# Adaptive-layernorm network with a chunked scan: half of each scan step's output projection moved into the step's own matrix work

## The chip, the core and the metric

The kernel runs on one NeuronCore of a Trainium2 chip. The core has a matrix engine (TensorE; PE in the profile, with its weight loads as PEld), a vector engine (VectorE, DVE), a scalar engine (ScalarE, ACT) and a general one (GpSimd, POOL). Each takes its own list of instructions in order and waits on semaphores; DMA queues move data beside them. The metric is the device time of one execution in microseconds. Before the change the median of three runs is 800.75 us (795.25 to 800.98).

## What is computed

Eight sequences of 512 tokens with 128 channels pass through two layers. Layer 0 is a state-space filter and a mixture of experts, layer 1 a chunked scan and a second mixture of experts. The change is in the scan of layer 1, and in the output projection that follows it:

```python
def step(carry, xs):                       # one chunk of 64 tokens
    W_in, W_out = carry
    qi, ki, vi, li, lo, wi, wo = xs
    p_q = softmax(einsum('bnhd,bDhd->bnhD', qi, W_in), axis=1)
    o = einsum('bnhD,bDhd->bnhd', p_q, W_out)
    p = softmax(einsum('bnhd,bDhd->bnhD', ki, W_in), axis=1)
    grad_out = einsum('bnhD,bnhd->bDhd', -p, vi)
    a = einsum('bDhd,bnhd->bnhD', W_out, vi)
    s = sum(p * a, axis=-1, keepdims=True)
    g_z = -(p * a - p * s)
    grad_in = einsum('bnhd,bnhD->bDhd', ki, g_z)
    W_in = wi * W_in - li * grad_in
    W_out = wo * W_out - lo * grad_out
    return (W_in, W_out), o
...
x = x + ga * (o @ Wo.T)                    # the projection that is split
```

## The kernel before

Everything is fp32 on 128 partitions. The eight sequences go in four pairs (`BP` = 4), each pair's 64-token chunk filling 128 partitions, so the scan has `T` = 32 steps: 8 chunks of 4 pairs, a chunk's four pairs one after the other. Each pair has its own states `w_in` and `w_out`. The first `TU` = 28 steps run in one software pipeline, written out by hand; the last four have no update and end apart. Each engine has a hand-written order of calls; nothing is scheduled by a program. The instruction list of the scan is unrolled.

PSUM is four banks of 1024 columns, `ps[0]` to `ps[3]`, all in use: `ps[0]` takes the values, then the output o, then `a`, then `grad_in`; `ps[1]` the half `[:, 0:128]` for the projection y, then q, then `grad_out`, then the turned values; `ps[2]` the turned keys, the turned `w_out`, then half of the logits; `ps[3]` k, the turned softmax weights, then the other half of the logits.

PE's loop over i runs in this order (in brackets the line of the profile): `y_of(i-3)`, the eight matmuls of the output projection of an earlier step (L1973); in three of four steps a small helper for the next chunk (`group_turn` L1892, `group_tokens` L1899, `group_sum` L1906 and L1909; none after step 21 or so, save one turn); `project` for the values and for q (L1918); `grad_in` (L1980); `k_turn` (L1951); `project` for k (L1918); `states_turn` (L1959); `states_q`, which makes o (L1966); `grad_out` (L1988); `p_turn`, the turn of the softmax weights (L1951); `a_of`, the pass of the values through `w_out` (L2009); `v_turn` (L1951); `logits_of` twice (L2018). Each fp32 matmul stands in the trace as two MATMUL and two LDWEIGHTS records, so the eight of `y_of` are x16. Those of 128x128 tiles are long, those of 64x64 tiles short.

Between a step's `a_of` and the next `project` of the values lies a loop through another engine: both write `ps[0]`, and DVE reads it in `weigh` (L1474), `mean` (L1478) and `difference` (L1482), which sets `am_done`. PE waits for it before that `project`, and POOL's `make_g` (L623) waits for it too, whose product `grad_in` needs.

DVE's order in one turn is `mean`, `difference`, `maxima` (L1443), `gate_y` (L1497), `group_rates_out` in one of four, `maxima`, `centre` twice (L1449), `add_up` (L1455), `update_in` (L1492), `q_silu` (L1433), `add_up`, `k_silu` (L1439), `invert` (L1462), `update_out` (L1487), in two of four a measurement for a layernorm (L1374 and L1378, or L1407 and L1412), `weigh`. POOL's is `scale_k` (L598), `normalise_p` twice (L619), `decay_out` (L584), `make_g` (L623), `decay_in` (L584), `add_y` (L628), `scale_v` (L598), with gathers and group work between. `gate_y` multiplies y by the gate into `y_gated`, and `add_y` adds it to x. ACT's `oT_of` (L989) copies o out of PSUM, and `w_outT_out` (L984) the turned states.

Of the kernel before, what the change touches and what calls it, by code (L numbers as in the profile page):

```python
# [5 lines left out]
ALU = mybir.AluOpType  # L6
# [7 lines left out]
P = 128  # L14
# [55 lines left out]
def program(nc, A):  # L70
    ctx = ExitStack()
    with ctx:
# [3 lines left out]
        def sem(name):  # L76
            return ctx.enter_context(nc.semaphore(name))
# [21 lines left out]
        def view(at, n, dt=F32):  # L99
# [106 lines left out]
        w_in = [view(23552 + 2048 * bp, 1024) for bp in range(BP)]  # L206
        w_out = [view(24576 + 2048 * bp, 1024) for bp in range(BP)]
        y_gated = small[:, 128:256]
        z_max = small[:, 256:288]
        z_sum, z_rec = ([small[:, 288 + 64 * k + 32 * u:320 + 64 * k + 32 * u] for u in range(2)] for k in range(2))  # L210
        s_sum, junk = small[:, 416:432], small[:, 432:433]
# [29 lines left out]
            sem(n) for n in ("z_centered", "z_summed", "pk_norm", "pq_norm", "silu_q", "silu_k", "g_done", "wout_new", "y_scaled", "win_new"))  # L241
        z_exp, vT_out, tanh_q, tanh_k, vtok_out, ktok_out, ptok_out, oT_out, woutT_out = (
            sem(n) for n in ("z_exp", "vT_out", "tanh_q", "tanh_k", "vtok_out", "ktok_out", "ptok_out", "oT_out", "woutT_out"))
        v_scaled, k_scaled, wout_dec, win_dec, x_added = (sem(n) for n in ("v_scaled", "k_scaled", "wout_dec", "win_dec", "x_added"))
        h_stored = [sem(f"h_stored{u}") for u in range(2)]
        lg_mm, tiles_counted, ex_done, oh_done, cnt_done, rhs_ready, ids_mm, gw = (
# [54 lines left out]
        def tile_of(t):  # L301

            return t % BP * NC + t // BP
# [12 lines left out]
        def y_bank(t):  # L316
            n = t - TU
            return ps[1][:, 0:C] if n < 0 else ps[2][:, n % 2 * 512:n % 2 * 512 + C]
# [142 lines left out]
        def _(pool):  # L461
# [144 lines left out]
            def scale_k(t):  # L606
                pool.wait_ge(ktok_out, t + 1)
                pool.wait_ge(group_rates, t // BP + 1)
                rate(k_tok, 0, t, k_scaled)
# [11 lines left out]
            def make_g(t):  # L621
                pool.wait_ge(am_done, t + 1)
                pool.tensor_tensor(g_tok, g_tok, p_tok, ALU.mult).then_inc(g_done, 1)  # L623

            def add_y(t):
                pool.wait_ge(y_scaled, t + 1)
                x = x_sb[:, tile_of(t) * C:(tile_of(t) + 1) * C]
                pool.tensor_tensor(x, x, y_gated, ALU.add).then_inc(x_added, 1)  # L628

# [21 lines left out]
            for i in range(-1, TU - 1):  # L651
                if 3 <= i and i + 17 < T:
                    gather_back(i + 17)
                if (c := group_of(i, 10, 3)) is not None:
                    group_add(c)
                if i >= 0:
                    scale_k(i)
                normalise_p(i + 1, 0, pq_norm)
                normalise_p(i + 1, 1, pk_norm)
                if i < 3:  # L660
                    gather_back(2 * i + 14)
                    gather_back(2 * i + 15)
                if i >= 0:
                    decay_out(i)
                if i >= 0:
                    make_g(i)
                if i >= 0:
                    decay_in(i)
                if i >= 0:
                    add_y(i)  # L670
                if (c := group_of(i, 12, 3)) is not None:
                    group_gate(c)
                if i >= 0:
                    scale_v(i)
                if (c := group_of(i, -11, 0, NC - 4)) is not None:
                    second_scale(c)
                if (c := group_of(i, -13, 0, NC - 4)) is not None:
                    second_shift(c)
            second_scale(NC - 4)
            scale_k(TU - 1)  # L680
            second_shift(NC - 4)
            normalise_p(TU, 0, pq_norm)
            decay_in(TU - 1)
# [411 lines left out]
        def _(dve):  # L1095
# [393 lines left out]
            def update_in(t):  # L1489
                dve.wait_ge(pe_gin, t + 1)  # L1490
                dve.wait_ge(win_dec, t + 1)
                dve.tensor_tensor(w_in[t % BP], w_in[t % BP], ps[0], ALU.add).then_inc(win_new, 1)  # L1492

            def gate_y(t):
                dve.wait_ge(pe_y, t + 1)
                after(dve, x_added, t)
                dve.tensor_tensor(y_gated, y_bank(t), rows1(GA, t % BP), ALU.mult).then_inc(y_scaled, 1)  # L1497
# [28 lines left out]
            for i in range(-1, TU - 1):  # L1526
# [26 lines left out]
                    group_measure(c)  # L1553
                if (c := group_of(i, -5, 0, NC - 2)) is not None:
                    second_measure(c)
                weigh(i + 1)
            mean(TU - 1)
            difference(TU - 1)
# [144 lines left out]
        def _(pe):  # L1703
# [265 lines left out]

            def y_of(t):  # L1970
                pe.wait_ge(oT_out, t + 1)
                for n in range(HP):
                    mm = pe.matmul(y_bank(t), oT_buffer(t)[:, n * P:(n + 1) * P], w_o[:, n * C:(n + 1) * C], start=(n == 0), stop=(n == HP - 1))  # L1973
                mm.then_inc(pe_y, 1)

            def grad_in(t):
                pe.wait_ge(g_done, t + 1)
# [109 lines left out]
            for i in range(2, TZ):  # L2087
# [42 lines left out]
                    grad_out(i - 3)  # L2130
                pe.wait_ge(silu_k, i + 1)
                p_turn(i - 2)
                a_of(i - 2)
                if i == 2:
                    pe.wait_ge(silu_q, i + 1)
# [1 line left out]
                v_turn(i - 2)  # L2137
                pe.wait_ge(silu_q, i + 1)
                pe.wait_ge(silu_k, i + 1)
                if i < TU:  # L2140
                    logits_of(i, 0)
                    after(pe, ptok_out, i - 1)
                    logits_of(i, 1)
                else:
                    last_logits(2 * i - TU)
                    if i < TZ - 1:
                        pe.wait_ge(ptok_out, i - 1)
                        last_logits(2 * i - TU + 1)
# [186 lines left out]
```

## Time and profile before

| | |
|---|---|
| median of three runs | 800.75 us (795.25 to 800.98) |
| the profiled execution, whole | 804.12 us |
| its span in the trace | 802.4 us |
| PE busy | 713.5 us, 89% of the span |
| PE weight loads busy | 655.1 us, 82% |
| DVE busy | 626.5 us, 78% |
| POOL busy | 580.9 us, 72% |
| ACT busy | 476.7 us, 59% |
| chain that ended last | PE 68%, DVE 10%, issue 8% |
| mean granted TensorE clock | 0.938 of full |

The scan of the 28 updated steps lies between about 161 us and 684 us. The trace gives for each instruction a start and a duration and, for idle time before it, what ended the wait; "issue" stands where the profile shows nothing that was waited for. Ends of matmuls are modelled, so lengths of PE's work are best read from one start to the next. A projection's x16 row and the next row's start, for example, tell what it took.

### The profile page before, as it was taken

How to read it: one execution, taken by the hardware profiler on the slowest of the kernel's cores; microseconds unless marked ns; L12 is line 12 of the kernel's file. 1: busy time of each engine (PE TensorE's matmuls, PEld its weight loads, DVE VectorE, ACT ScalarE, POOL GpSimd, SP SyncE). 2: the span in 40 equal slices, each digit the busy share in tenths (PEclk: the TensorE clock that was granted, in tenths of full speed). 3: DMA queues.
4: the chain of work that ended last, by engine and by line, in shares of the span. 5: the costliest groups of instructions: out<-in, count | busy, mean ns of one | idle time of the engine just before them, and what ended most of it. 6: DMA issues, size and time to landing. Idle time of an engine off the chain costs nothing.

```text
span 802.4 us, 34232 instructions
## 1 busy us (share of the span) xinstructions
PE 713.5 (89%) x14919; PEld 655.1 (82%) x14920; DVE 626.5 (78%) x1033; ACT 476.7 (59%) x774; POOL 580.9 (72%) x433
## 2 busy tenths in 40 slices
PE   5679798678899999999999999999999999877997
PEld 5357587577799989898888989898988889776897
DVE  6594645379789989899898999999998899866205
ACT  5673244238755756686676678667657775641930
POOL 7630377276979898889888988889787888832750
PEclk8695689979999999999999999999999999986999
DMA  8402334310520000000000000000000000061127
GB/s 324 197 28 77 102 77 103 69 30 9 160 68 14 6 7 7 10 7 7 7 7 7 19 4 2 18 3 3 3 17 4 3 15 18 5 227 65 52 82 273
DMA packets 33584, 42.89 MB, mean 53 GB/s; under 512 B 4001, under 2 KB 25649, under 8 KB 32929
## 3 DMA queue, kind: packets, MB, share of 16 engines
q1 hardware_dynamic: 29856, 33.99, 12.6%
q0 software_dynamic: 3296, 6.76, 3.5%
q8 instruction: 117, 1.92, 1.0%
q14 instruction: 27, 0.21, 0.1%
q10 hardware_dynamic: 288, 0.01, 0.0%
HBM read 26.65 MB, written 14.09 MB: 51 GB/s over the span
## 4 chain that ended last, share of the span: by engine, by line
PE 68%; DVE 10%; issue 8%; ACT 6%; DMA 5%; POOL 2%; POOLq 0%; ACTq 0%; SPq 0%; DVEq 0%
PE psum L1918 19%; PE psum L1973 7%; PE psum L1951 7%; PE psum L2018 7%; PE psum L2009 4%; PE psum L1966 4%; PE psum L1980 4%; PE psum L1988 3%; DMA arena<-h_rows,route 2%; PE psum L1959 2%; ACT arena L1076 2%; POOL arena L560 2%; PE psum L2276 2%; ACT arena L1086 1%; PE psum L1777 1%
## 5 line engine op out<-in xcount | busy, mean ns | idle before, releaser
L1918 PE MATMUL psum<-hT,w_qkv 128*128 128x128 f32 x1408 | 176.3, 283 | 2.6 <-DVE arena L1395 1.4
L1918 PEld LDWEIGHTS psum<-hT,w_qkv 128*128 128x128 f32 x1408 | 166.7, 196 | 5.8 <-DVE arena L1395 1.6
L619 POOL TENSOR_TENSOR arena<-arena,small 128x1024 f32<-128x1024 f32 x56 | 106.0, 1914 | 41.2 <-DVE small L1462 41.2
L598 POOL TENSOR_TENSOR arena<-arena 128x1024 f32<-128x1024 f32 x56 | 106.6, 1904 | 10.6 <-ACT arena L973 10.4
L584 POOL TENSOR_TENSOR arena<-arena 128x1024 f32<-128x1024 f32 x56 | 106.6, 1904 | 0.1
L1455 DVE TENSOR_REDUCE small<-arena 128x16 f32<-128x1024 f32 x60 | 73.0, 1217 | 8.9 <-ACT arena L962 6.8
L623 POOL TENSOR_TENSOR arena<-arena 128x1024 f32<-128x1024 f32 x28 | 65.9, 2355 | 13.5 <-DVE arena L1482 13.5
L1443 DVE TENSOR_REDUCE small<-psum 128x16 f32<-128x1024 f32 x60 | 72.7, 1213 | 0.0
L1449 DVE TENSOR_TENSOR arena<-psum,small 128x1024 f32<-128x1024 f32 x60 | 70.4, 1212 | 0.1
L942 ACT ACTIVATE arena<-psum 128x1024 f32<-128x1024 f32 x28 | 28.7, 1024 | 69.6 <-PE psum L1918 69.6
L560 POOL DMA_INDIRECT arena<-h_rows,route x39 | 39.6, 1016 | 39.7 <-issue 38.4
L1951 PE MATMUL psum<-arena 64*128 64x64 f32 x1344 | 61.8, 230 | 6.7 <-issue 3.9
L2018 PE MATMUL psum<-arena 64*64 64x128 f32 x1792 | 61.5, 279 | 5.6 <-issue 2.8
L1973 PE MATMUL psum<-w_o,arena 128*128 128x128 f32 x512 | 65.1, 281 | 0.6 <-ACT arena L989 0.6
L962 ACT ACTIVATE arena<-arena 128x1024 f32<-128x1024 f32 x60 | 62.9, 1051 | 4.5 <-DVE arena L1449 4.2
L1973 PEld LDWEIGHTS psum<-w_o,arena 128*128 128x128 f32 x512 | 60.0, 193 | 4.5 <-issue 3.4
L1951 PEld LDWEIGHTS psum<-arena 64*128 64x128 f32 x1344 | 49.4, 139 | 12.8 <-issue 3.9
L2018 PEld LDWEIGHTS psum<-arena 64*64 64x64 f32 x1792 | 51.9, 136 | 9.6 <-issue 7.4
L947 ACT ACTIVATE arena<-psum 128x1024 f32<-128x1024 f32 x28 | 28.7, 1025 | 36.1 <-PE psum L1951 31.9
L1474 DVE TENSOR_TENSOR arena<-arena,psum 128x1024 f32<-128x1024 f32 x28 | 34.0, 1216 | 18.6 <-PE psum L2009 18.2
L546 POOL DMA_INDIRECT arena<-o_rows,route x32 | 33.1, 1034 | 19.9 <-DMA o_rows<-arena 13.2
L875 ACT ACTIVATE arena<-psum,route 128x128 f32<-128x128 f32 x78 | 21.3, 380 | 41.9 <-PE psum L1856 41.9
(332 smaller groups left out, 1625.6 us busy)
## 6 DMA issues: line engine op xcount, KB each, us to landing
y_rows<-hT SPq DMA_DIRECT2D x8, 512.0 KB
arena<-in_L_W_rows SPq DMA_DIRECT2D x2, 2048.0 KB, 11.3
arena<-y_rows SPq DMA_DIRECT2D x8, 512.0 KB, 8.8
o_rows<-arena SPq DMA_DIRECT2D x9, 256.0 KB
x_sb<-in_x_rows SPq DMA_DIRECT2D x4, 512.0 KB, 6.0
arena<-in_L_W_rows SPq DMA_DIRECT2D x2, 1024.0 KB, 9.9
arena<-in_W_in_rows SPq DMA_DIRECT2D x4, 512.0 KB, 14.9
arena<-in_W_out_rows SPq DMA_DIRECT2D x4, 512.0 KB, 9.6
```

Of the source, the lines that this page charges most:

```text
L584: pool.tensor_tensor(w4, w4, d4.unsqueeze(3).to_broadcast([P, 2, HP, D]), ALU.mult).then_inc(done, 1)
L598: pool.tensor_tensor(x3, x3, lr[:, tile_of(t) * 32 + k * H:tile_of(t) * 32 + k * H + H].unsqueeze(2).to_broadcast([P, H, D]), ALU.mult).th ...
L619: pool.tensor_tensor(z4, z4, r3.unsqueeze(3).to_broadcast([P, 8, 2, CH]), ALU.mult).then_inc(done, 1)
L623: pool.tensor_tensor(g_tok, g_tok, p_tok, ALU.mult).then_inc(g_done, 1)
L962: act.activation(z, z, ACT.Exp, scale=0.5).then_inc(z_exp, 1)
L1443: dve.tensor_reduce(z_max[:, 16 * jh:16 * jh + 16], h3(ps[2 + jh]), AX_X, ALU.max).then_inc(z_maxed, 1)
L1449: dve.tensor_tensor(h3(zs[t % 2][:, jh * 1024:(jh + 1) * 1024]), h3(ps[2 + jh]), z_max[:, 16 * jh:16 * jh + 16].unsqueeze(2).to_broadcast( ...
L1455: dve.tensor_reduce(z_sum[t % 2][:, 16 * jh:16 * jh + 16], h3(zs[t % 2][:, jh * 1024:(jh + 1) * 1024]), AX_X, ALU.add).then_inc(z_added, 1)
L1918: mm = pe.matmul(ps[bank][:, p * P:(p + 1) * P], w_qkv[:, j * HD + p * P:j * HD + (p + 1) * P], hT[:, at:at + P], start=True, stop=True)
L1951: mm = pe.transpose(out[:, col((r, 2), (n, HP))], of[half(r), at(n):at(n) + P], eye[half(r), :])
L1973: mm = pe.matmul(y_bank(t), oT_buffer(t)[:, n * P:(n + 1) * P], w_o[:, n * C:(n + 1) * C], start=(n == 0), stop=(n == HP - 1))
L2018: mm = pe.matmul(out, w_in[t % BP][half(r), col((be, 2), (p, HP))], x4[half(r), :, p, be, :], start=True, stop=True)
```

## The change

In steps below `TU` the output projection is split. `y_of` does the second four of its eight matmuls, at its old place and into its old bank. A new `early_y_of` does the first four between `p_turn` and `a_of` of the step itself, into `ps[2][:, 0:C]`, after ACT has copied the turned states out of that bank. DVE's new `gate_early_y` multiplies this half by the gate into a new buffer `early_gated` (128 columns of SBUF), ahead of `weigh`. POOL's new `add_early_y` adds it to x, between `scale_k` and `normalise_p`; `add_y` then adds the second half. PE waits for `early_scaled` before `logits_of` writes the bank again. Three semaphores of layer 0 are used anew.

```diff
+        early_gated = sb("early_gated", [P, C])[:, :]
...
+        early_y, early_scaled, early_added = a0_up, a0_scaled, a0_sq
...
+            def add_early_y(t):
+                pool.wait_ge(early_scaled, BP + t + 1)
+                x = x_sb[:, tile_of(t) * C:(tile_of(t) + 1) * C]
+                pool.tensor_tensor(x, x, early_gated, ALU.add).then_inc(early_added, 1)
+
             def add_y(t):
                 pool.wait_ge(y_scaled, t + 1)
+                pool.wait_ge(early_added, BP + min(t + 1, TU))
...
                     scale_k(i)
+                if i >= 0:
+                    add_early_y(i)
                 normalise_p(i + 1, 0, pq_norm)
...
             scale_k(TU - 1)
+            add_early_y(TU - 1)
...
+            def gate_early_y(t):
+                dve.wait_ge(early_y, BP + t + 1)
+                dve.wait_ge(early_added, BP + t)
+                dve.tensor_tensor(early_gated, ps[2][:, 0:C], rows1(GA, t % BP), ALU.mult).then_inc(early_scaled, 1)
...
+                gate_early_y(i + 1)
                 weigh(i + 1)
...
             def y_of(t):
                 pe.wait_ge(oT_out, t + 1)
-                for n in range(HP):
-                    mm = pe.matmul(y_bank(t), oT_buffer(t)[:, n * P:(n + 1) * P], w_o[:, n * C:(n + 1) * C], start=(n == 0), stop=(n == HP - 1))
+                n0 = HP // 2 if t < TU else 0
+                for n in range(n0, HP):
+                    mm = pe.matmul(y_bank(t), oT_buffer(t)[:, n * P:(n + 1) * P], w_o[:, n * C:(n + 1) * C], start=(n == n0), stop=(n == HP - 1))
                 mm.then_inc(pe_y, 1)
+
+            def early_y_of(t):
+                pe.wait_ge(oT_out, t + 1)
+                pe.wait_ge(woutT_out, t + 1)
+                for n in range(HP // 2):
+                    mm = pe.matmul(ps[2][:, 0:C], oT[:, n * P:(n + 1) * P], w_o[:, n * C:(n + 1) * C], start=(n == 0), stop=(n == HP // 2 - 1))
+                mm.then_inc(early_y, 1)
...
                 p_turn(i - 2)
+                early_y_of(i - 2)
                 a_of(i - 2)
...
                 pe.wait_ge(silu_k, i + 1)
+                pe.wait_ge(early_scaled, BP + i - 1)
                 if i < TU:
                     logits_of(i, 0)
```

PE's order of the kernel before, in a step in the middle of the scan, from `grad_out` to the next step's projections of the values and of q:

```order
L1988 MATMUL psum<-arena 64x64 x32
L1951 MATMUL psum<-arena 128x64 x16
L2009 MATMUL psum<-arena 64x64 x32
L1951 MATMUL psum<-arena 128x64 x16
L2018 MATMUL psum<-arena 64x2x64 x32
L1892 MATMUL psum<-ident,arena 128x128 x4
L1973 MATMUL psum<-w_o,arena 128x128 x8
L1918 MATMUL psum<-hT,w_qkv 128x128 x16
```

The same place after the change, where L1998 is `early_y_of`, L1991 `y_of`, L2034 `a_of` and L2043 `logits_of`:

```order
L2013 MATMUL psum<-arena 64x64 x32
L1968 MATMUL psum<-arena 128x64 x16
L1998 MATMUL psum<-w_o,arena 128x128 x4
L2034 MATMUL psum<-arena 64x64 x32
L1968 MATMUL psum<-arena 128x64 x16
L2043 MATMUL psum<-arena 64x2x64 x32
L1909 MATMUL psum<-ident,arena 128x128 x4
L1991 MATMUL psum<-w_o,arena 128x128 x4
L1935 MATMUL psum<-hT,w_qkv 128x128 x16
```

Four long matmuls have gone from behind the logits to a place ahead of `a_of`, of the step before in the pipeline's count; the number of matmuls is the same.

DVE's order of the kernel before around `weigh` (L1474), in a step with a layernorm measurement:

```order
L1462 RECIPROCAL small<-small 128x32
L1487 TENSOR_TENSOR arena<-arena,psum 128x1024
L1374 BN_STATS small<-x_sb 128x6 x4
L1378 BN_AGGR small<-small 128x2 x4
L1474 TENSOR_TENSOR arena<-arena,psum 128x1024
L1478 TENSOR_REDUCE small<-arena 128x16
L1482 TENSOR_TENSOR arena<-psum,small 128x1024
```

The same place after the change, where L1508 is `gate_early_y` and L1485 `weigh`:

```order
L1473 RECIPROCAL small<-small 128x32
L1498 TENSOR_TENSOR arena<-arena,psum 128x1024
L1385 BN_STATS small<-x_sb 128x6 x4
L1389 BN_AGGR small<-small 128x2 x4
L1508 TENSOR_TENSOR early_gated<-psum,mod 128x128
L1485 TENSOR_TENSOR arena<-arena,psum 128x1024
L1489 TENSOR_REDUCE small<-arena 128x16
L1493 TENSOR_TENSOR arena<-psum,small 128x1024
```

One small operation is new, just ahead of `weigh`; `gate_y` stays where it was.

## Rows read from the trace of the kernel before

**Rows 1.** Windows of every engine: start:end, length, busy time of each (instructions), clock, DMA.

```profile
241.03:598.06 357.03, 343.50 (x9083) 320.42 (x9081) 331.40 (x417) 244.31 (x323) 313.73 (x189) 1.00 0.03 8
598.06:684.68 86.62, 82.89 (x2311) 77.59 (x2309) 78.78 (x85) 56.58 (x67) 73.41 (x44) 1.00 0.04 10
```

**Rows 2.** PE's timeline, step from 598 us: start, length, line, operation, count, [idle before].

```profile
598.06 2.05 PE L1973 MATMUL psum<-w_o,arena 128*128 128x128 f32 x16
599.95 3.74 PE L1918 MATMUL psum<-hT,w_qkv 128*128 128x128 f32 x32
603.61 1.16 PE L1980 MATMUL psum<-arena 64*64 64x64 f32 x64
...
610.65 1.04 PE L2009 MATMUL psum<-arena 64*64 64x64 f32 x56
612.58 0.34 PE L2009 MATMUL psum<-arena 64*64 64x64 f32 x8 [0.88 <-issue]
612.85 0.72 PE L1951 MATMUL psum<-arena 64*128 64x64 f32 x16
...
615.40 0.66 PE L1892 MATMUL psum<-ident,arena 128*128 128x128 f32 x4
615.90 0.72 PE L1973 MATMUL psum<-w_o,arena 128*128 128x128 f32 x5
```

**Rows 3.** PE's timeline, the other two helpers and what follows them.

```profile
421.46 1.00 PE L1899 MATMUL psum<-arena,hT 128*128 128x64 f32 x8
422.31 3.79 PE L1918 MATMUL psum<-hT,w_qkv 128*128 128x128 f32 x32
...
439.99 0.39 PE L1906 MATMUL psum<-arena 128*128 128x128 f32 x2
...
440.69 0.49 PE L1918 MATMUL psum<-hT,w_qkv 128*128 128x128 f32 x2
```

**Rows 4.** Waits from 220 to 690 us: total us, times, longest us.

```profile
PE psum L2009 <- issue: 7.4, 11, 1.1
...
PE psum L1951 <- issue: 3.9, 7, 0.8
PE psum L2018 <- issue: 2.8, 6, 0.6
...
PE psum L1988 <- issue: 1.8, 2, 1.2
```

**Rows 5.** PE's timeline at two gaps that follow each other.

```profile
290.30 0.21 PE L1951 MATMUL psum<-arena 64*128 64x64 f32 x1 [0.68 <-issue]
...
294.06 0.87 PE L2018 MATMUL psum<-arena 64*64 64x128 f32 x19 [0.36 <-issue]
```

**Rows 6.** Window of every engine between those two gaps, columns as in rows 1.

```profile
290.30:294.06 3.76, 3.40 (x126) 2.89 (x126) 2.42 (x3) 2.05 (x2) 3.76 (x3) 1.00 0.02 4
```

**Rows 7.** The page's part on DMA queues: packets, MB, share.

```profile
q8 instruction: 117, 1.92, 1.0%
```

**Rows 8.** DVE's timeline, weigh, difference and gate_y in four steps.

```profile
435.66 1.22 DVE L1474 TENSOR_TENSOR arena<-arena,psum 128x1024 f32<-128x1024 f32 x1 [1.49 <-PE psum L2009]
...
438.17 1.22 DVE L1482 TENSOR_TENSOR arena<-psum,small 128x1024 f32<-128x1024 f32 x1
...
453.34 1.19 DVE L1474 TENSOR_TENSOR arena<-arena,psum 128x1024 f32<-128x1024 f32 x1
...
470.12 1.22 DVE L1474 TENSOR_TENSOR arena<-arena,psum 128x1024 f32<-128x1024 f32 x1 [1.14 <-PE psum L2009]
...
475.51 0.29 DVE L1497 TENSOR_TENSOR small<-psum,mod 128x128 f32<-128x128 f32 x1 [0.53 <-PE psum L1973]
...
505.65 1.22 DVE L1474 TENSOR_TENSOR arena<-arena,psum 128x1024 f32<-128x1024 f32 x1 [0.82 <-PE psum L2009]
```

**Rows 9.** POOL's timeline, add_y in one step and make_g in another.

```profile
424.85 0.46 POOL L628 TENSOR_TENSOR x_sb<-x_sb,small 128x128 f32<-128x128 f32 x1
...
439.47 2.35 POOL L623 TENSOR_TENSOR arena<-arena 128x1024 f32<-128x1024 f32 x1 [0.66 <-DVE arena L1482]
```

## The prediction

> **What bounds the kernel now.** I read first the windows of all engines over the scan, cut at the starts of `y_of`. From 241.03 to 598.06 us lie 20 steps, from there to 684.68 five more [rows 1]. A step takes 357.03 / 20 = 17.85 us in the first stretch and 86.62 / 5 = 17.32 in the second, at full clock. PE is busy for 96% of both; DVE is next with 331.40 / 357.03 = 93%. So PE sets the step, and DVE has little over a microsecond to spare.
>
> Next I read PE's timeline of a single step [rows 2]. The step starts with `y_of` at 598.06, the projections of v and q start at 599.95, `a_of` at 610.65, `v_turn` at 612.85, and the logits end at 615.40. `a_of` is cut in two: after 56 of its 64 records PE stood still for 0.88 us, and "issue" means that nothing waited for is seen. `grad_in`, 64 records of the same shape, takes 1.16 at 603.61, some 0.06 of it beside the block behind. So `a_of` would take 1.10, and here it takes 2.20: the stop costs 1.10. Without it the step is 17.34 - 1.10 = 16.24. The helpers add 0.50 (615.40 to 615.90), 0.85 and 0.70 [rows 2, 3] in three of four steps, 0.51 on average. So a step in the first stretch would be 16.75 without stops, against 17.85 found: **1.10 us of each step is such a stop.**
>
> What is it? The list of waits shows where the stops stand: 7.4 us at `a_of`, 2.8 at the logits, 3.9 at the turns, 1.8 at `grad_out` [rows 4], all in the stretch of short matmuls, none at the projections. Two stops that follow each other, at 290.30 and 294.06, each fall inside a block [rows 5], and between them PE took 126 matmul and 126 load records [rows 6]. The queue q8 moved 117 packets of code and 1.92 MB, which is 16 KB a packet [rows 7]. My reading is that a packet holds the next 252 records and a few waits, and that a stop is PE at the end of one packet before the next is in. The stretch from one such stop to the next took 3.76 us, its end stop included. A run that holds a projection takes longer: `project` needs 3.66 / 2 = 1.83 us for 32 records (599.95 to 603.61), against 1.10 for the 128 of `grad_in`. There are no stops at the projections.
>
> The Trainium skill, "Runtime: NRT & Kernel Launch", section "Instruction fetch mechanics", says that each engine's instruction memory is refilled in 16 KiB blocks of 256 instructions while it runs, which these rows agree with, and that the crossing is mostly hidden because the sequencer dispatches more slowly than the blocks arrive. By that half of the rule there is nothing for the change to take away, and the sum below would lose its only gain; rows 5 and 6 do not agree with it for short matmuls, but it is the third rival.
>
> **The change part by part.**
>
> Four matmuls (8 matmul and 8 load records) move from the slow stretch to the middle of the dense one. Half of 1.89 is 0.95 us [rows 2]. A run that holds them takes 0.95 longer, so a stop at its end shrinks by up to 0.95; the stops are 1.10 a step, and the run that `y_of` leaves has the projections and stays long. Not all stops lie behind the new place. Those at `grad_out` (1.8) lie ahead of it, and of the 3.9 at the turns I take 3.2 as `p_turn`'s, ahead of it too (rows do not part `p_turn` from `v_turn`; 0 and 3.9 are the bounds). That is 5.0 of 15.9, 31%. So of 1.10 some 0.34 stay, and 0.02 for stops over 0.95: **0.36 left, 0.74 taken**. Bounds: 0.1 left, or all 1.10.
>
> PE gets three more waits and a second accumulation group. No row shows their price here. Below, nothing; above, 0.32, four times the 0.08 of a semaphore that has to come from another engine (below). I take 0.1 a step, near nothing, since what they wait for is done.
>
> DVE gets one 128x128 operation, 0.29 us as `gate_y` [rows 8]; I take 0.28 a step. POOL gets one of 0.46 us [rows 9]. It is busy for 313.73 of 357.03 us [rows 1], so it has 2.16 idle a step, and what stands behind the new place, `normalise_p`, is used by PE only in the next step. I cost it at nothing; with that cover gone it would be up to 0.46 a step. ACT and the DMA queues get nothing.
>
> **The cover that goes.** PE's next `project` of the values waits for `am_done`. `difference` ends at 438.17 + 1.22 = 439.39, 3.73 behind the start of `weigh` at 435.66 [rows 8]. A semaphore between engines costs 0.08: `make_g`, which waits for the same one, starts at 439.47 [rows 9]. With two of them PE may start 3.9 us after the end of `a_of`. Before, PE had 2.55 (turn and logits, 612.85 to 615.40) and 1.89 (`y_of`) to do, 4.44 and more. Now it has 2.55 + 0.95 = 3.50 and the helper. So a step without a helper waits 0.4 us for DVE, and with a late DVE more. If `weigh` is late by L, PE starts at the greater of 3.50 + helper and 3.90 + L after the end of `a_of`. From that start to the end of the next `a_of` is 10.70 (599.95 to 610.65) + 1.10 + 0.95 = 12.75, plus 0.36 and 0.1, 13.21.
>
> How late DVE is comes from its own work between two `weigh`. The four steps of [rows 8], without the waits for PE, are: with the rates and a measurement 453.34 - 435.66 = 17.68; bare 16.78 - 1.14 = 15.64; the next two 35.53 - 0.53 - 0.82 = 34.18, 17.09 each. With 0.28: 17.96, 15.92, 17.37, 17.37. The waits for `y_of` in `gate_y` go, since half a projection ends sooner.
>
> Four steps in a row, L = 0 at first:
> - helper 0.70: PE starts at 4.20, step 17.41; DVE late by 17.96 - 17.41 = 0.55.
> - no helper: 3.90 + 0.55 = 4.45, step 17.66; DVE catches up.
> - helper 0.50: 4.00, step 17.21; DVE late by 0.16.
> - helper 0.85: 4.35, step 17.56; DVE catches up.
>
> The mean is 69.84 / 4 = 17.46, a gain of 0.39 a step: of 0.74 taken from the stops nearly half goes to DVE and the handshake. Over 20 steps that is 7.8. The five steps behind have almost no helper: 3.90 + 13.21 = 17.11 each, 85.55 against 86.62, a gain of 1.1. The three steps ahead of 241 us are of the first stretch's kind: 1.0. The sum is **9.9 us**. The profiled execution took 804.12, so 794.2; in the same ratio the median of 800.75 becomes **791**.
>
> **The rivals.**
>
> *More relief or less coupling.* If all stops went, the same four steps give 17.31 and 16.75 for bare ones: 10.8 + 2.9 + 1, about 15 us, 786. If the stops are as I say but DVE never holds PE up, a step is 16.75 + 0.46 = 17.21 and a bare one 16.70: 12.8 + 3.1 + 1, about 17, 784. Both together 775. For it: DVE's waits inside a step [rows 8] may shrink further. Against: DVE at 93% now, and at 96% of a step of 17.5.
>
> *The relief is there and is eaten.* Single stops go up to 1.2 us [rows 4] and some steps have none, and DVE's load from 15.6 to 17.7; my four steps use the mean stop. Where a stop and a light step meet, nothing is won. If that costs 0.25 a step, the gain is 4 us: 797.
>
> *Slower: the code fetch is not what stops PE, or a packet costs its fixed time anyway.* Then 1.10 stays, the shorter cover counts, and PE goes from start to end of `a_of` in 12.75 + 1.10 + 0.1 = 13.95. With the same rules steps are 18.15, 17.85, 17.95 and 18.30, mean 18.06, 0.21 worse; bare ones 17.85, 0.53 worse: 4.2 + 2.6 = 6.8, **807.5**. This is decided by the relief: from 0.25 us a step down the change loses. Against it: 252 records between two stops [rows 6] and none at the slow blocks.
>
> **How the numbers follow.** Forecast (787 to 795) 0.50, more relief (775 to 786) 0.18, eaten (795 to 802) 0.20, slower (802 to 812) 0.12. A measurement can tell about 1% from no change, which is 8 us: below 792.7 is faster, above 808.8 slower. Three quarters of the forecast and all of the first rival are below: 0.55. Half of the last is above: 0.06. The rest, 0.39, is within. The range leaves out the farthest of both sides: 780 to 803.
>
> **What would show it.** In the timeline of PE the new four matmuls take 0.95 us and the stops behind them nearly vanish, while those at `grad_out` and `p_turn` stay; their total falls from 1.10 to about 0.36 a step. A new wait of PE at the projection of the values (the line of `project`), released by DVE's `difference`, of about 0.4 in steps without a helper. DVE's wait before `weigh` is mostly gone, and its busy share rises to 96%. `gate_y` no longer waits for `y_of`. No wait of PE at the logits for the early gate. Wrong would be: stops as long as before, or a wait at the logits.

## The result, and the profile after

The changed kernel takes 817.83 us, median of four runs (815.67 to 818.78), against 800.6 us for the kernel before. The ratio is 1.0224, with a 95% interval of 1.0183 to 1.0266: 2.2% slower. The forecast was 791 us in a range of 780 to 803, so it was wrong in sign. Even the rival that had it slower ended at 812.

In the profiled executions the span grew from 802.4 to 817.0 us, by 14.6. The windows of every engine, cut at the same places as [rows 1], show where. First the kernel before, its ending (the last four scan steps) and all that follows; columns are start:end, length, busy time of PE, PEld, DVE, ACT, POOL with instructions, granted clock, DMA.

```profile
684.68:699.32 14.64, 11.33 (x424) 10.29 (x421) 13.76 (x24) 9.77 (x15) 11.61 (x8) 1.00 0.02 4
699.32:802.40 103.08, 86.00 (x751) 81.42 (x751) 44.97 (x116) 41.43 (x117) 41.52 (x41) 0.89 0.39 136
```

The same windows of the changed kernel, with its 20 and 5 steps ahead of them:

```profile
241.25:603.08 361.83, 346.95 (x9085) 322.08 (x9081) 337.18 (x437) 245.38 (x322) 319.58 (x209) 1.00 0.03 8
603.08:690.32 87.24, 83.81 (x2313) 77.76 (x2309) 79.83 (x91) 57.14 (x69) 75.63 (x49) 1.00 0.03 6
690.32:709.97 19.65, 12.67 (x412) 11.50 (x412) 15.70 (x24) 10.36 (x15) 14.71 (x10) 0.79 0.06 16
709.97:817.00 107.03, 91.50 (x751) 87.30 (x751) 44.14 (x116) 41.47 (x117) 41.63 (x41) 0.85 0.38 131
```

The 20 steps took 361.83 us for 357.03 [rows 1], 18.09 a step for 17.85. The five behind took 87.24 for 86.62, the ending 19.65 for 14.64. The rest took 107.03 for 103.08; that part is not the change's, since in a second pair of traces from one chip (e0 and e7 below) it is 104.5 before and 104.0 after.

The waits of the changed kernel between 220 and 700 us (total, times, longest):

```profile
POOL x_sb L630 <- DVE early_gated L1508: 54.7, 25, 3.5
...
DVE arena L1485 <- PE psum L2034: 17.6, 24, 3.4
PEld psum L2005 <- issue: 15.1, 20, 3.8
...
PE psum L2005 <- issue: 11.2, 12, 3.7
...
PEld psum L1968 <- DVE arena L1450: 3.6, 16, 0.5
...
PEld psum L1935 <- DVE arena L1493: 2.4, 6, 0.4
```

Against [rows 4], the stops at `a_of` (now L2034) and at the logits (L2043) no longer stand near the top of PE's waits. PE now waits ahead of `grad_in` (L2005), where [rows 4] has nothing. At the top is GpSimd, standing 54.7 us at the new addition (L630) for VectorE's new gate.

One step of the changed kernel shows how these hang together. These are GpSimd, the new gate, the weigh behind it and TensorE, from the timeline:

```profile
454.99 1.16 PE L1998 MATMUL psum<-w_o,arena 128*128 128x128 f32 x8
...
456.08 1.16 PE L2034 MATMUL psum<-arena 64*64 64x64 f32 x64
...
456.79 0.26 DVE L1508 TENSOR_TENSOR early_gated<-psum,mod 128x128 f32<-128x128 f32 x1
...
457.31 1.22 DVE L1485 TENSOR_TENSOR arena<-arena,psum 128x1024 f32<-128x1024 f32 x1 [0.26 <-PE psum L2034]
457.35 0.46 POOL L630 TENSOR_TENSOR x_sb<-x_sb,early_gated 128x128 f32<-128x128 f32 x1
457.77 3.78 POOL L621 TENSOR_TENSOR arena<-arena,small 128x1024 f32<-128x1024 f32 x2
...
461.10 1.16 PE L1935 MATMUL psum<-hT,w_qkv 128*128 128x128 f32 x8 [0.22 <-DVE arena L1493]
461.52 1.89 POOL L586 TENSOR_TENSOR arena<-arena 128x1024 f32<-128x1024 f32 x1
```

GpSimd's two `normalise_p` (L621) begin only when the early half has been multiplied, gated and added. Behind them come `decay_out` (L586) and `make_g`. In this step GpSimd was busy with its own work until 457.35 and did not stand at the addition. In the step before it did, for 1.97 us, and that step shows what it does to TensorE:

```profile
439.29 0.46 POOL L630 TENSOR_TENSOR x_sb<-x_sb,early_gated 128x128 f32<-128x128 f32 x1 [1.97 <-DVE early_gated L1508]
439.71 3.78 POOL L621 TENSOR_TENSOR arena<-arena,small 128x1024 f32<-128x1024 f32 x2
443.45 1.90 POOL L586 TENSOR_TENSOR arena<-arena 128x1024 f32<-128x1024 f32 x1
...
445.31 2.36 POOL L625 TENSOR_TENSOR arena<-arena 128x1024 f32<-128x1024 f32 x1
...
447.77 1.16 PE L2005 MATMUL psum<-arena 64*64 64x64 f32 x64 [0.61 <-issue]
```

`make_g` (L625) ends at 447.67 and `grad_in` starts at 447.77. In the kernel before, `make_g` of the same step started at 439.47 after an idle time of 0.66 [rows 9] and ended at 441.82, over two microseconds before it was needed. Over the 20 steps `make_g` ends 2.42 us ahead of `grad_in` on average in the kernel before; in the changed kernel `grad_in` starts 0.10 us behind it in 17 of 20 steps.

In the ending nothing hides this:

```profile
690.32 1.16 PE L1991 MATMUL psum<-w_o,arena 128*128 128x128 f32 x8
...
694.96 2.35 POOL L625 TENSOR_TENSOR arena<-arena 128x1024 f32<-128x1024 f32 x1
...
697.41 1.98 PE L2005 MATMUL psum<-arena 64*64 64x64 f32 x64 [3.66 <-issue]
```

TensorE stood 3.66 us for `make_g`, and the granted clock of the ending's window is 0.79, where it was 1.00 before. Cut finer, it is 1.00 until the wait has begun and 0.50 (the 1.2 GHz level) behind it. Columns are start:end, length, busy time of PE with instructions, granted clock, DMA:

```profile
692.00:694.00 2.00, 1.16 (x64) 1.00 0.04 8
...
697.40:699.30 1.90, 1.89 (x64) 0.50 0.00 0
```

The 64 records of `grad_in` took 1.98 us instead of 1.16. Of the 5.01 us that the ending grew, 3.06 lie ahead of the start of `grad_in` (7.09 us from the ending's start for 4.03), and 1.95 between it and the logits behind it (5.03 for 3.08), where the same work ran at the lower clock.

The table sets 20 steps of each kernel side by side. Each figure is the mean length of a block in us, from its start to the next block's start in PE's timeline, so a wait counts to the block ahead of it. The last column is e1, below.

| block of a step | before | changed | e1 |
|---|---|---|---|
| projection y, both halves | 1.86 | 2.15 | 2.12 |
| v and q, and waits ahead of `grad_in` | 3.71 | 4.18 | 3.74 |
| `states_q` and `grad_out`, and waits ahead of the turn | 2.10 | 2.37 | 2.51 |
| `p_turn`, `a_of`, `v_turn`, logits | 5.27 | 4.48 | 4.44 |
| everything else | 4.91 | 4.91 | 4.91 |
| step | 17.85 | 18.09 | 17.72 |

### The profile page after: what moved, and what is told of

Same layout as the page of the kernel before. It is cut to its first block, busy times and chain, and to the rows that moved or that the text cites. A ratio compares the mean times of both kernels' runs of the same rounds, so it can differ in the third digit from the quotient of the medians.

```text
span 817.0 us, 34402 instructions
## 1 busy us (share of the span) xinstructions
PE 722.5 (88%) x14919; PEld 661.4 (81%) x14920; DVE 635.7 (78%) x1061; ACT 479.0 (59%) x774; POOL 592.1 (72%) x461
## 4 chain that ended last, share of the span: by engine, by line
POOL 40%; issue 20%; PE 19%; DVE 13%; ACT 5%; DMA 3%; POOLq 0%; ACTq 0%; DVEq 0%; SPq 0%
POOL arena L600 10%; POOL arena L621 10%; POOL arena L586 8%; POOL arena L625 4%; PE psum L1725 2%; POOL arena L562 2%; POOL arena L548 2%; ACT arena L1087 2%; PE psum L2303 2%; DMA arena<-h_rows,route 2%; DVE small L1454 1%; ACT arena L1097 1%; PE psum L1991 1%; PE psum L1794 1%; PE psum L2075 1%
## 5 line engine op out<-in xcount | busy, mean ns | idle before, releaser
L1935 PEld LDWEIGHTS psum<-hT,w_qkv 128*128 128x128 f32 x1408 | 164.4, 194 | 9.4 <-DVE arena L1493 2.4
L621 POOL TENSOR_TENSOR arena<-arena,small 128x1024 f32<-128x1024 f32 x56 | 106.1, 1915 | 2.5 <-DVE small L1473 2.5
L586 POOL TENSOR_TENSOR arena<-arena 128x1024 f32<-128x1024 f32 x56 | 106.7, 1905 | 0.1
L625 POOL TENSOR_TENSOR arena<-arena 128x1024 f32<-128x1024 f32 x28 | 66.1, 2361 | 0.0
L2043 PE MATMUL psum<-arena 64*64 64x128 f32 x1792 | 58.3, 278 | 2.8 <-DVE arena L1450 2.6
L630 POOL TENSOR_TENSOR x_sb<-x_sb,early_gated 128x128 f32<-128x128 f32 x28 | 12.8, 457 | 60.6 <-DVE early_gated L1508 60.6
L2043 PEld LDWEIGHTS psum<-arena 64*64 64x64 f32 x1792 | 50.6, 136 | 5.4 <-issue 3.5
L1485 DVE TENSOR_TENSOR arena<-arena,psum 128x1024 f32<-128x1024 f32 x28 | 34.2, 1220 | 18.5 <-PE psum L2034 18.5
L2005 PE MATMUL psum<-arena 64*64 64x64 f32 x1792 | 33.3, 224 | 13.9 <-issue 11.2
```

Of the source, the lines that this page charges most:

```text
L586: pool.tensor_tensor(w4, w4, d4.unsqueeze(3).to_broadcast([P, 2, HP, D]), ALU.mult).then_inc(done, 1)
L621: pool.tensor_tensor(z4, z4, r3.unsqueeze(3).to_broadcast([P, 8, 2, CH]), ALU.mult).then_inc(done, 1)
L1935: mm = pe.matmul(ps[bank][:, p * P:(p + 1) * P], w_qkv[:, j * HD + p * P:j * HD + (p + 1) * P], hT[:, at:at + P], start=True, stop=True)
L2043: mm = pe.matmul(out, w_in[t % BP][half(r), col((be, 2), (p, HP))], x4[half(r), :, p, be, :], start=True, stop=True)
```

## The experiments

Twelve more runs were made, in three groups. Each was compared with the kernel before in its own group. In two of the three groups the kernel before took 832.5 us, in the other 801.8; the scan's steps hardly differ, so ratios and steps are compared, not totals.

### e1: GpSimd's addition behind its other work

```diff
-                if i >= 0:
-                    add_early_y(i)
                 normalise_p(i + 1, 0, pq_norm)
...
                 if i >= 0:
+                    add_early_y(i)
                     add_y(i)
```

The last step's call moves in the same way. All kernels from e4 to e11 that have the split have this order too, save e7.

> The changed kernel with one call of GpSimd moved: the addition of the early half stands behind the decay of w_in, just ahead of add_y, instead of ahead of normalise_p. Theory A (GpSimd's queue): in the changed kernel GpSimd stands 2.2 us a step at that addition (54.7 us in 25 waits), and normalise_p, decay and make_g queue behind it, so that grad_in on TensorE waits. Then this kernel loses that wait: the wait before grad_in goes from 26 us to a few, steps fall from 18.1 to about 17.5 us, the ending after the last step is as in the kernel before, and the time is 789 to 797 us. Theory B (the shorter cover ahead of the projection of the values, and VectorE's extra gate): that part is unchanged here, so the time stays at 812 to 818 us.

Measured: 1.0028 of the kernel before (0.9995 to 1.0062), and 1.0004 (0.9970 to 1.0037) when it ran again as e11. The 20 steps:

```profile
262.97:617.33 354.36, 347.08 (x9081) 322.10 (x9081) 332.39 (x435) 245.10 (x320) 320.38 (x207) 1.00 0.03 8
```

A step is 17.72 us, and the ending takes 15.15. So theory A holds for the loss against the kernel before: moving one call of GpSimd takes back about 2%. The wait ahead of `grad_in` is gone (second row of the table). But 17.72 is not the 17.5 that I expected, and the time is no better than before. Something else takes the rest.

Most of it is in the third row, 2.51 for 2.10. Read from the starts of TensorE's records, this 0.41 has three parts: 0.15 is a wait for `k_silu` ahead of the turn, 0.08 is for the most part longer stops in `grad_out`, and 0.18 is `states_q` itself, where stops stand in five steps that the kernel before does not have. One of them, with the gather on GpSimd beside it:

```profile
307.29 1.04 POOL L548 DMA_INDIRECT arena<-o_rows,route  x1
...
308.63 0.55 PE L1982 MATMUL psum<-arena 64*64 64x64 f32 x21 [0.40 <-issue]
```

Each of the five ends about 0.3 us behind the end of such a gather. The kernel before and the changed kernel have as many gathers in these steps and no stop of this kind. Its cause is open.

### e2: the wait alone, in the kernel before

```diff
                     scale_k(i)
+                    pool.wait_ge(pe_a, i + 1)
                 normalise_p(i + 1, 0, pq_norm)
```

The same wait stands behind the last `scale_k`.

> The kernel before with one wait added and no work: GpSimd waits, at the place where the changed kernel's addition stood, for TensorE's a_of of the same step. Theory A: this alone makes make_g late, grad_in waits on TensorE, and the kernel is 8 to 20 us slower than before, 809 to 821 us, also in its ending. Theory B: GpSimd has 2.2 us idle a step, and the wait fits into it: 800 to 803 us.

Measured: 1.0149 (1.0073 to 1.0224), 12 us slower. The waits and the 20 steps:

```profile
POOL arena L619 <- PE psum L2011: 68.4, 27, 5.0
```

```profile
263.08:625.18 362.10, 346.32 (x9085) 322.05 (x9081) 334.00 (x419) 245.60 (x323) 312.98 (x189) 1.00 0.03 8
```

A wait with no work behind it makes steps of 18.10 us and an ending of 19.5 us, against 18.09 and 19.65 in the changed kernel, with a wait of 3.70 us at the same `grad_in` in the ending. For the ending this shows the first cause from both sides: taking the held-up queue away from the changed kernel cures it, adding it to the kernel before brings it. For the 20 steps 18.10 against 18.09 is a coincidence. Here the second row of the table is only 0.11 longer (3.82), the third 0.26 (2.36), most of it the same kind of stop in `states_q` as in e1, and the fourth 0.14 shorter (5.13). `make_g` is late here too, but TensorE still has the whole of `y_of` and its stops to do between `a_of` and `grad_in`, and comes there 5.16 us behind `am_done`; in e1, where it waits for nobody there, it comes after 4.21. So in the steps the late `make_g` reaches `grad_in` nearly every time only together with the shorter cover of the split.

Nor does e2 part the wait from the 0.46 us of work. GpSimd's `normalise_p` begins on average 2.07 us ahead of the end of `a_of` in the kernel before, 0.15 behind it in the changed kernel and 0.11 behind it in e2. Of these 2.2 us the addition's work is at most 0.46; the rest is standing and waiting.

### e3: four matmuls more, nothing moved

```diff
                 p_turn(i - 2)
+                idle_y_of(i - 2)
                 a_of(i - 2)
```

`idle_y_of` is `early_y_of` without a signal; nobody reads what it makes.

> The kernel before with four 128x128 matmuls more a step, at the place of the early half and into the same bank; nothing reads their product, and the output projection is whole at its old place. They are 0.95 us of TensorE a step, 26.6 us in all. Theory F (a stop is TensorE at the end of a 16 KB packet of its code): the stops behind the new place shrink by as much as the work adds, so the cost is 0.2 to 0.4 us a step, 5 to 11 us: 806 to 812 us. Rival: stops have a fixed price, or are caused by something else, and the work adds its full length: 820 to 827 us.

Measured: 1.0204 (1.0136 to 1.0272), 17 us. Neither number fits. The 20 steps:

```profile
264.15:629.54 365.39, 361.91 (x9241) 338.58 (x9241) 329.60 (x415) 242.85 (x320) 311.33 (x187) 1.00 0.03 8
```

A step is 18.27 us, 0.42 more, and the added block takes 1.11, not 0.95. So 0.69 of 1.11 was paid for by stops that went: `a_of` fell from 1.53 to 1.15, `p_turn` and `v_turn` from 1.56 together to 1.36, the logits from 2.18 to 2.02. Work that is put in and costs 38% of its length on the path had idle time there to fill, which the rival of a fixed price doesn't allow.

That the idle time is the fetch of code rests on the traces. Counting TensorE's records and its waits together, the 20 steps of the kernel before pass 72 places at which another 256 are full. All 24 of its stops stand at such places, none elsewhere, and each ends 1.2 to 1.7 us behind the landing of a 16 KB packet of q8. From start to start these stops add up to 18.4 us, 0.92 a step; in e3 they are 4.7 us, without any new wait of TensorE. In e1 and e2 the stops in `states_q` stand at none of these places.

DVE showed the second cause here: it waited 30.1 us for `a_of`, in 25 waits.

```profile
DVE arena L1474 <- PE psum L2015: 30.1, 25, 2.3
```

### e4: the early half ahead of the turn

```diff
-                p_turn(i - 2)
                 early_y_of(i - 2)
+                p_turn(i - 2)
                 a_of(i - 2)
```

> As e1_add_late, and the early half stands ahead of the turn of the softmax weights, behind grad_out, instead of behind that turn. Theory F: the packets that end in that turn now hold long matmuls too, so the stops at the turn go as well (about 3 of the 16 us seen in the kernel before), while TensorE waits some 0.3 us a step for ScalarE's copy of o, which was just done in time: within 4 us of e1_add_late on either side. Rival: if the place makes no difference to the stops, it is the wait of 0.3 us a step alone, 8 us slower than e1_add_late.

Measured: 1.0071 (1.0035 to 1.0106), 17.88 us a step. `p_turn` is 0.64 for 0.66 in e1, so next to nothing was left to win there, and the waits ahead grew by more: `states_q` and `grad_out` take 2.62 for 2.51. It is the cost side that came out, 3.6 us behind e1: just within the 4 of theory F and half of the rival's 8, so it decides little.

### e0 and e7: both kernels again on one chip

> The kernel before, unchanged, for its trace on the chip of this group of runs. If the stops of TensorE come from the fetch of its code, they stand in the same blocks as in the first trace of this kernel, and about 1.1 us a step, on any chip: 20 steps take 355 to 360 us. Differences in the time of the whole kernel then lie ahead of the scan.

> The changed kernel, unchanged, beside the others on this chip. If GpSimd's place in its queue is what costs most, the ratio to the kernel before is 1.018 to 1.027 again, and e1_add_late's 1.003 is 1.5 to 2% better. If the first ratio was the chip's, it is near 1.003.

Measured: e0 has the 20 steps in 356.47 us, 17.82 each, with its stops in the same blocks (`a_of` 1.51, logits 2.19). Its waits between 260 and 700 us, as [rows 4]:

```profile
PE psum L2009 <- issue: 6.7, 9, 1.1
...
PE psum L1951 <- issue: 3.7, 7, 0.9
...
PE psum L2018 <- issue: 2.8, 7, 0.6
```

e7 is 1.0229 (1.0183 to 1.0275) of the kernel before, so the result is not one chip's. Its 20 steps take 364.20, its ending 20.2.

### e5: the early half ahead of the wait for k_silu

```diff
+                early_y_of(i - 2)
                 pe.wait_ge(silu_k, i + 1)
                 p_turn(i - 2)
-                early_y_of(i - 2)
                 a_of(i - 2)
```

> As e1_add_late, with the early half of the projection directly behind grad_out, ahead of TensorE's wait for k_silu. Theory L (a loop through VectorE): in e1_add_late, VectorE ends k_silu, TensorE turns the weights, does the early half (1.09 us) and a_of, and only then can VectorE go on with weigh; VectorE stands 14 us in 24 waits there and TensorE 0.4 us a step at the turn for k_silu. With the early half ahead of that wait it is out of this loop: TensorE's wait at the turn is filled by it, and steps fall from 17.72 to 17.3 to 17.5 us: 5 to 10 us faster than e1_add_late, 0.993 to 1.000 of the kernel before. Rival: the loop does not bind, and only the wait for ScalarE's copy of o is added, as in e4_half_sooner: 1.003 to 1.007 of the kernel before.

Measured: 1.0034 (1.0003 to 1.0065), 355.81 us for 20 steps, 17.79 each. Theory L's numbers failed. The half is out of the loop, but in its waits stands another:

```profile
PEld psum L1997 <- ACT arena L999: 9.1, 22, 0.4
...
PE psum L1997 <- ACT arena L999: 6.0, 22, 0.3
```

TensorE now waits for ScalarE's copy of o, in nearly every step: `grad_out` and this wait take 1.49 for 1.11 in e0. With `states_q` it is 2.47 for 2.51 in e1, where the wait for k_silu and the stops in `states_q` stood. So e5 exchanged these for another wait of the same size. Its ratio is the rival's, but it takes the half out of the loop only by putting it behind ScalarE, and so doesn't tell whether the loop binds.

### e6: the early half behind a_of

```diff
-                early_y_of(i - 2)
                 a_of(i - 2)
+                early_y_of(i - 2)
```

and on VectorE `gate_early_y` behind `weigh`.

> As e1_add_late, with the early half directly behind a_of, and its gate on VectorE behind weigh. The half is out of the loop k_silu, turn, a_of, weigh too, and TensorE again has 4.4 us of its own work between a_of and the next projection of the values. Theory L: the wait at the turn and the one ahead of the projection go, 0.3 to 0.5 us a step; but the stops inside a_of itself (7.4 of 16 us) come back. So 17.5 to 17.8 us a step, 0.996 to 1.004 of the kernel before. Rival: the loop does not bind, and the returned stops make it 5 to 10 us slower than e1_add_late, 1.009 to 1.015.

Measured: 1.0075 (1.0044 to 1.0107), 17.96 us a step, between the two expectations. The stops inside `a_of` are back (1.59 for 1.10), as in the kernel before:

```profile
PE psum L2033 <- issue: 8.1, 12, 1.0
```

`grad_out` and the wait at the turn did shrink, to 1.24 from 1.35 in e1. Of the four places tried with GpSimd's call moved (e1, e4, e5, e6), none is faster than the kernel before.

### e8 and e9: a shorter loop on VectorE, with and without the split

```diff
-                dve.tensor_reduce(s_sum, h3(g_tok), AX_X, ALU.add).then_inc(mean_step, 1)
+                dve.tensor_reduce(s_sum, h3(g_tok)[:, :, 0:4], AX_X, ALU.add).then_inc(mean_step, 1)
```

`mean` sums 4 of 64 columns here, so the kernel leaves out part of what it has to compute; `mean` takes 0.22 us instead of 1.22.

> e1_add_late with VectorE's loop made about 1 us shorter: mean sums 4 of each head's 64 columns in place of all 64 (this leaves part of the computation out). Theory L (in the split kernel VectorE's loop from weigh over k_silu, the turn, the early half and a_of to the next weigh sets the step): TensorE's waits at the turn for k_silu (0.41 us a step in e1_add_late) and ahead of the projection of the values (0.4 in steps without a helper) vanish, steps fall from 17.72 to 17.2 to 17.35 us, and the kernel takes 0.984 to 0.990 of the kernel before. Rival (the loop does not bind; the split has a price on TensorE itself): steps stay at 17.6 to 17.7, 0.997 to 1.002.

> The kernel before with the same shortened mean, as the control of e8_split_short_mean. Theory L: here the stops of TensorE set the step and VectorE is a microsecond ahead of need, so a shorter VectorE loop gives 0 to 0.15 us a step: 0.995 to 1.000 of the kernel before. If it gives as much as in the split kernel, VectorE's loop bound both, and the stops were hidden behind it.

Measured: e8 0.9947 (0.9918 to 0.9977), e9 0.9992 (0.9960 to 1.0023). Their 20 steps, e8 first:

```profile
260.37:610.42 350.05, 344.90 (x9081) 320.97 (x9081) 316.00 (x436) 243.02 (x320) 320.26 (x207) 1.00 0.03 8
```

```profile
259.93:616.70 356.77, 344.26 (x9083) 320.75 (x9081) 312.50 (x418) 243.72 (x323) 313.58 (x190) 1.00 0.03 8
```

In the kernel before, a microsecond less on VectorE gives nothing (17.84 a step for 17.85 and 17.82). In the split kernel it gives 0.23 (17.50 for 17.73 in e11, on the same chip). The ratio 0.9947 lies between the two expectations, and the step is longer than I expected (17.2 to 17.35). TensorE's waits for VectorE did go, at the turn (0.15) and ahead of the projection of the values (0.06 in the first row, 0.03 in the second): the split has made VectorE's loop a bound that it was not. But this is not all that changed. The stops in `states_q` beside gathers went too, some 0.14, for a reason that isn't shown, and the stops for code came back by about as much (8.2 us in 20 steps for 5.3 in e11), presumably since TensorE no longer waits while its code comes. 0.23 for the split of the projection stays. The control isn't clean either: in e9 about 0.1 us a step of stops off the places of the code came in, and about as much of the others went.

The loop can be read in a step of e1 without a helper. TensorE's turn waits for `k_silu` (L1449), then comes the early half (L1997), then `a_of` (L2033), and only then can VectorE `weigh` (L1484):

```profile
627.90 1.21 DVE L1449 SCALAR_TENSOR_TENSOR arena<-arena,psum 128x1024 f32<-128x1024 f32 x1
...
629.16 0.71 PE L1967 MATMUL psum<-arena 64*128 64x64 f32 x16 [0.23 <-DVE arena L1449]
...
629.81 1.16 PE L1997 MATMUL psum<-w_o,arena 128*128 128x128 f32 x8
...
630.90 1.16 PE L2033 MATMUL psum<-arena 64*64 64x64 f32 x64
...
632.13 1.22 DVE L1484 TENSOR_TENSOR arena<-arena,psum 128x1024 f32<-128x1024 f32 x1 [0.83 <-PE psum L2033]
```

From the end of `k_silu` at 629.11 to `weigh` are 3.02 us. Of these the early half is 1.09, and VectorE is idle for 0.83 of them, until `a_of` is done.

### e10: a quarter instead of a half

```diff
-                n0 = HP // 2 if t < TU else 0
+                n0 = HP // 4 if t < TU else 0
...
-                for n in range(HP // 2):
+                for n in range(HP // 4):
```

> As e1_add_late, but two of the eight matmuls are moved instead of four. The loop through VectorE grows by 0.6 us instead of 1.1, and TensorE has 2.55 + 1.4 = 4.0 us of its own between a_of and the projection of the values, so the wait there goes. Stops shrink by 0.47 at most instead of 0.94. Theory L: the handshakes lose more than the stops come back, 17.5 to 17.7 us a step, 0.994 to 1.001. Rival: what counts is the stops alone; then it is 0.2 to 0.3 us a step slower than e1_add_late, 1.008 to 1.011.

> e1_add_late, unchanged, on this chip beside the other three, in more rounds: 0.998 to 1.004 of the kernel before, as its first interval says.

Measured: e10 0.9993 (0.9972 to 1.0014), 17.71 us a step; e11 1.0004. The quarter keeps more stops (`a_of` 1.25 for 1.10) and loses as much less in waits. Neither can be told from the kernel before; e10 is in the range of theory L, and its rival's 1.008 to 1.011, 0.2 to 0.3 us a step slower than e1, is excluded. The early block of two matmuls takes 0.65 us, where half of the four's 1.09 would be 0.55.

## Why the prediction was wrong

**What bounds the kernel** was right. The stops stood where it put them, in a second trace too (e0), and the blocks with stops fell from 5.27 to 4.48 us a step: 0.79, where the sum had 0.74; in e3, without new waits, 0.75. Counted gap by gap the stops fell from 0.92 a step, not 1.10, to 0.26. The size was right, the places were not: I let the stops of `p_turn` and `grad_out` stay, and those of `p_turn` fell from 3.6 us in 20 steps to 1.0, while those in `grad_out` rose from 1.4 to 3.5. The rival in which the stops stay was wrong, though it alone had the sign.

**The step that failed** is GpSimd's, "I cost it at nothing; with that cover gone it would be up to 0.46 a step". It had two faults. It priced the addition's work and its idle time, but not its wait: the addition stands in the queue at a place that GpSimd reached, in 19 of the 20 steps, before the early half was multiplied and gated, in some of them 1.3 us before TensorE had begun it. And it asked who uses `normalise_p`, which is indeed needed only in the next step, and not who uses what is queued behind that: `decay_out` and `make_g`, which `grad_in` of the same turn needs. The price was 0.47 us a step in the second row of the table (there together with the shorter cover, as e2 shows) and 5.0 us in the ending, 1.95 of them by the lower clock behind the wait. Ahead of the 20 steps, from the first `y_of` on, the changed kernel took 3.6 us more in the pair on one chip (42.34 for 38.71 in e7 and e0) and 1.0 more in the first pair (40.86 for 39.89). The ending was no term of the sum at all. Moving this call took the kernel from 1.0224 and 1.0229 to 1.0028 and 1.0004, so its place accounts for the whole of the measured loss; what else the split costs and gives cancels.

**The cover that goes** was right where it was worked out and incomplete. In the changed kernel the step from 459.72 waits for `am_done`, and `y_of` with this wait takes 1.38 us (459.72 to 461.10), where it takes 1.00 without a wait: 0.4, as forecast. But the path "from that start to the end of the next `a_of`", 12.75 us, was taken to have no wait in it. The turn of the softmax weights waits for `k_silu`, and the early half lies between that turn and `weigh`, inside VectorE's loop. The chain I wrote down began at `weigh` and ended at `am_done`, the half of the loop without the new work. Measured in e1, the wait at the turn is 0.15 us a step. The other 0.26 of the third row are stops, 0.18 of them in `states_q` beside GpSimd's gathers, which no term of the sum had and whose cause is open. VectorE, forecast to be busy for 96% and hardly to wait ahead of `weigh`, is busy for 93% (337.18 of 361.83) and waits there for `a_of` for 17.6 us in 24 waits: the early half has made `a_of` later for it.

**The waits and the second group** had 0.1 us a step and cost 0.26 to 0.29 (first row of the table), of which 0.05 to 0.08 is the wait for `am_done`. The early four matmuls take 1.08 to 1.13 us in every place tried, and the late four 0.89 to 1.00. Half a projection is not half the price.

**The gate on VectorE** was sized rightly, 0.26 to 0.29 us, and TensorE never stood at the logits for it.

With the first fault mended, e1, the sum reads: 0.83 a step saved on stops, 0.26 paid for the split, 0.41 in the third row, 0.03 ahead of `grad_in`. That leaves 0.13 of a forecast 0.39, and over the whole kernel nothing that can be measured.

## What to carry to other kernels

A new wait costs the queue behind it, not the work beside it. Before pricing it, write down the instructions behind it up to the first that another engine needs soon, and ask when the awaited signal comes in the same turn, not in the one before. And work that fills one engine's idle time is free only if it lies outside every loop through a second engine: list each handshake from that engine's last product to its next input, with the new work inside. And a control that brings back the same loss hasn't shown the same cause until the loss stands in the same blocks: e2 had the step's total to 0.01 us and another sum behind it.

## What the runs showed of the hardware

Between two stops of TensorE in the dense stretch lie 252 records in 3.76 us [rows 6], one 16 KB packet of its code [rows 7]. All 24 stops in 20 steps stand where another 256 records and waits are full, each ends 1.2 to 1.7 us behind the landing of a packet, and together they cost 0.92 us of each step of 17.85. Four long matmuls put into the stretch cost 0.42 us for 1.11 of work (e3). By the Trainium skill, "Runtime: NRT & Kernel Launch", section "Instruction fetch mechanics", crossing a block is mostly hidden; 48 of 72 crossings are here, but in the dense stretch of 64x64 tiles many are not, and there the measurement decides.

A block of four 128x128 matmuls among short ones takes 1.09 us, the late four ahead of a projection 0.89 behind a helper of long matmuls and 1.00 behind the logits: some 0.2 between the extremes. The cause of that 0.2 was not looked for.

TensorE stops inside `states_q`, with 0.4 to 0.6 us from one start to the next, 0.2 to 0.3 us behind the end of a GpSimd gather of 1.04 us, in five of e1's 20 steps and, with nothing but a wait added to GpSimd, in seven of e2's. In the same steps of the kernel before and of the changed kernel, with as many gathers, there is none. What brings it about is open.

In the wait of 3.66 us near the end of the scan the granted clock fell from 1.00 to 0.50, and stayed there for 6.8 us (694.92 to 701.75): `grad_in` took 1.98 us for 1.16. In e7 it was the same (698.04 to 704.87). In the kernel before and in e1, without the wait, the ending ran at 1.00 throughout. So the wait cost 3.06 us by itself and 1.95 by the clock behind it.
